# Projecting a mixer's tokens once and moving the half for the next token down a row by a transfer

## What is computed

```python
proj = u @ w_in.T                      # z, x, B, C, and the small columns dt, A, trap, angles
...
alpha = exp(A_t * dt_t)
beta  = (1 - tr_t) * dt_t * alpha      # share of the token before
gamma = tr_t * dt_t                    # share of the token itself
base  = bt * (px * beta + xt * gamma)  # px: x of the token before (0 at the first)
sr = sr * alpha + concat([base[..., :R] * cos(th), base[..., R:]])
si = si * alpha + base[..., :R] * sin(th)
y  = sum((sr[..., :R] * cos(th) + si * sin(th)) * ct[..., :R]) + sum(sr[..., R:] * ct[..., R:])
carry = (sr, si, xt)
...
out = (y + D * x) * silu(z) @ w_out.T
```

## Time and profile before

| what | value |
|---|---|
| median of 3 runs | 615.77 us (612.55 to 616.32) |
| the profiled execution | 614.08 us |
| its span in the profile | 612.4 us |
| PE busy | 557.5 us, 91% of the span |
| DVE, ACT, POOL busy | 437.5, 279.8, 229.2 us |
| mean clock of PE, of full speed | 0.974 |

### The profile page before, as it was taken

The page is one execution under the profiler, slowest core; times in us unless marked ns, Lnnn a source line. Parts: engine busy times, 40 slices in busy tenths (PEclk is TensorE's granted clock), DMA queues, the critical chain, the costliest instruction groups (busy, mean ns, idle before and its releaser), DMA issues. The chain is left out here.

```text
span 612.4 us, 17980 instructions
## 1 busy us (share of the span) xinstructions
PE 557.5 (91%) x6440; PEld 466.4 (76%) x6440; DVE 437.5 (71%) x1079; ACT 279.8 (46%) x548; POOL 229.2 (37%) x288
## 2 busy tenths in 40 slices
PE   5679999999999667999999998987999999999994
PEld 5658887888888455787788777775888888888883
DVE  2846777776787458687787787563877977977963
ACT  2357656656665324575475564453333333333220
POOL 2234246426634574325435526733031131131122
PEclk9989999999999976999999999998999999999998
DMA  7123122122211463545545638005274275265260
GB/s 227 48 85 99 42 70 69 47 63 68 61 51 35 127 188 103 151 138 149 160 131 145 162 83 231 9 7 124 52 173 113 63 172 116 61 170 113 48 155 18
DMA packets 52562, 63.21 MB, mean 103 GB/s; under 512 B 6208, under 2 KB 32480, under 8 KB 52496
## 3 DMA queue, kind: packets, MB, share of 16 engines
q1 hardware_dynamic: 50320, 59.35, 36.3%
q0 software_dynamic: 704, 1.92, 1.1%
q10 hardware_dynamic: 1472, 1.05, 0.7%
HBM read 49.26 MB, written 11.21 MB: 99 GB/s over the span
## 5 line engine op out<-in xcount | busy, mean ns | idle before, releaser
L1209 ACT ACTIVATE prob<-bank 128x512 f32<-128x512 f32 x128 | 69.4, 595 | 42.5 <-PE bank L1463 33.5
L1305 DVE TENSOR_REDUCE nmax<-bank 128x4 f32<-128x512 f32 x112 | 71.9, 684 | 22.5 <-PE bank L1463 21.1
L1998 PE MATMUL bank<-xT_hl_c,w_up 128*128 128x512 f32 x288 | 85.3, 419 | 2.9 <-ACTq L67 2.9
L1915 ACT ACTIVATE sg<-bank 128x512 f32<-128x512 f32 x72 | 43.1, 598 | 93.7 <-PE bank L1998 88.5
L2009 PEld LDWEIGHTS bank<-w_down,hid 128*128 128x128 f32 x576 | 73.9, 191 | 10.7 <-DVE hid L1955 4.4
L2009 PE MATMUL bank<-w_down,hid 128*128 128x128 f32 x576 | 76.4, 276 | 2.3 <-DVE hid L1955 1.5
L1453 PE MATMUL bank<-neg_i,mask 64*128 64x256 bf16 x512 | 51.5, 280 | 10.2 <-issue 3.4
L1998 PEld LDWEIGHTS bank<-xT_hl_c,w_up 128*128 128x128 f32 x288 | 49.5, 192 | 9.8 <-issue 3.1
L788 POOL TENSOR_TENSOR w_tok<-xg 128x256 f32<-128x256 f32 x32 | 23.8, 745 | 88.1 <-DVE xg L859 62.7
L1955 DVE TENSOR_TENSOR hid<-gu,share 128x512 f32<-128x512 f32 x64 | 47.8, 747 | 5.5 <-DMA share<-cw_scratch 3.4
L1951 DVE TENSOR_TENSOR gu<-sg,bank_pair 128x512 f32<-128x512 f32 x48 | 32.8, 683 | 22.0 <-ACT sg L1915 15.0
(11 more groups left out here) (213 smaller groups left out, 1197.2 us busy)
## 6 DMA issues: line engine op xcount, KB each, us to landing
share<-cw_scratch SPq DMA_DIRECT2D x64, 256.0 KB, 5.6
rows<-sum_rows_scratch SPq DMA_DIRECT2D x32, 256.0 KB, 3.2
k_stack<-k_scratch SPq DMA_DIRECT2D x32, 128.0 KB, 2.9
q_stack<-q_scratch SPq DMA_DIRECT2D x32, 128.0 KB, 2.8
k_scratch<-k_part SPq DMA_DIRECT2D x16, 192.0 KB, 2.4
q_scratch<-q_part SPq DMA_DIRECT2D x16, 192.0 KB, 2.4
x<-xT_in SPq DMA_DIRECT2D x8, 256.0 KB, 8.0
mask<-mask_in SPq DMA_DIRECT2D x8, 256.0 KB, 3.1
```

The costliest lines, as they stand in the source:

```text
L1209: act.activation(prob[:, b % 2, ORDER[n], :, :], (TT0, TT1)[n % 2][:, :], ACT.Exp, scale=XD ** -0.5)\
L1305: dve.tensor_reduce(nmax[:, b, 4 * u:4 * u + 4], (SS0, SS1)[n % 2][:, :].rearrange("p (i k) -> p i k", i=4), AX_X, ALU.max, negate=True).t ...
L1915: act.activation(sg[:, k, :], GG[k][:, :], ACT.Silu).then_inc(a_s.sem, 1)
L1998: mm = pe.matmul(bank[:, :], w_up[:, which, a, c, :], xT_hl[par][:, v, :], start=(n == 0), stop=(n == 2))
```

## The change

The tokens are projected once. `tokens` works on a pair q of sequences (2q, 2q + 1) with three matmuls each, and a bank holds both. DVE makes two products of 512 columns a pair: `xnext`, the tokens times the share that the next token has in them, and `w_tok`, the tokens times their own share. A DMA moves `xnext` down by one partition into `prev` (rows 0 to 126 to rows 1 to 127; row 0 of `prev` stays cleared). POOL adds `prev` to `w_tok`, 512 columns a pair. `w_tok` now holds all four sequences of a group; `prev` and `xnext` exist once.

So that DVE can multiply with the next token's share, `beta` is moved up by one row once, by a DMA of 127 rows of 512 B (`shares[:, 1]`), for which POOL makes the coefficients of the second half before the first causal selections. The cleared column of `xhl` and the wait for it go. SP issues the two moves of a group: the one of pair 1 after the first sum row of the next group, that of the next group's pair 0 after the fourth.

```diff
-        shares = sb("shares", [P, NSEQ, 2, HEADS])
-        gamma, beta = shares[:, :, 0, :], shares[:, :, 1, :]
+        shares = sb("shares", [P, 2, NSEQ, HEADS])
+        gamma, beta = shares[:, 0], sb("beta", [P, NSEQ, HEADS])
...
-        xhl = sb("xhl", [P, 2, 2, GS, P + 1], F32R)
+        xhl = sb("xhl", [P, 2, 2, GS, P], F32R)
+        prev = sb("prev", [P, 2, D_INNER])
...
-                pe.wait_ge(s_zero, 1)
...
-                dve.memset(xhl[:, :, :, :, 0:1].bitcast(F32), 0.0).then_inc(s_zero, 1)
+                dve.memset(prev[0:1, :, :], 0.0)
+                dve.memset(shares[:, 1], 0.0)
...
-        xg = sb("xg", [P, 2, 2, D_INNER])
-        w_tok = sb("w_tok", [P, 2, D_INNER])
+        w_tok = sb("w_tok", [P, GS, D_INNER])
+        xnext = sb("xnext", [P, 2, D_INNER])
...
+            sp.wait_ge(s_share, 6)
+            sp.dma_start(shares[0:P - 1, 1], beta[1:P]).then_inc(s_later, 16)
             sp.wait_ge(s_stored, 32)
+            for loaded in s_prev:
+                loaded.prime(sp)
+
+            def load_prev(g, q):
+                sp.wait_ge(s_xg.sem, s_xg.at(g, 2 * q))
+                sp.sem_inc(sp_passed, 1)
+                sp.wait_ge(s_w.sem, s_w.at(g, q - 1))
+                sp.dma_start(prev[1:P, :, :], xnext[0:P - 1, :, :]).then_inc(s_prev[q].sem, 16)
...
                 if left:
-                    for b in range(GS):
+                    load_row(sp, g + 1, 0)
+                load_prev(g, 1)
+                if left:
+                    for b in range(1, GS):
                         load_row(sp, g + 1, b)
+                    load_prev(g + 1, 0)
...
+            load_prev(0, 0)
             pairs(sp, group)
...
-            def inputs_of(g, b):
-
-                pool.wait_ge(s_xg.sem, s_xg.at(g, b))
-                pool.wait_ge(s_y.sem, s_y.at(g, b - 2))
-                pool.tensor_tensor(w_tok[:, b % 2, :], xg[:, b % 2, 0, :], xg[:, b % 2, 1, :], ALU.add).then_inc(s_w.sem, 1)
+            def inputs_of(g, q):
+
+                pool.wait_ge(s_xg.sem, s_xg.at(g, 2 * q + 1))
+                pool.wait_ge(s_prev[q].sem, s_prev[q].at(g))
+                w = w_tok[:, 2 * q:2 * q + 2, :]
+                pool.tensor_tensor(w, w, prev[:, :, :], ALU.add).then_inc(s_w.sem, 1)
...
-                inputs_of(g, 2)
-                if left:
-                    for b in range(GS - 1):
+                if left:
+                    causal(pool, g + 1, 0)
+                inputs_of(g, 1)
+                if left:
+                    for b in range(1, GS):
                         causal(pool, g + 1, b)
                 else:
                     part_third(pool, a, 0, 1)
-                inputs_of(g, 3)
-                if left:
-                    causal(pool, g + 1, GS - 1)
+                if left:
...
-                    for b in range(2):
-                        inputs_of(g + 1, b)
+                    inputs_of(g + 1, 0)
...
+            coefficients(pool, 1)
+            betas(pool, 1)
             for b in range(2):
                 causal(pool, 0, b)
-            coefficients(pool, 1)
-            betas(pool, 1)
...
-            def inputs_of(g, b):
-
-                dve.wait_ge(s_xx.sem, s_xx.at(g, b))
-                dve.wait_ge(s_w.sem, s_w.at(g, b - 2))
-                dve.tensor_tensor(xg[:, b % 2, :, :].rearrange("p s (h e) -> p (s h) e", h=HEADS),
...
+            def inputs_of(g, q):
+
+                dve.wait_ge(s_xx.sem, s_xx.at(g, q))
+                dve.wait_ge(s_prev[1 - q].sem, s_prev[1 - q].at(g - 1 + q))
+                for s, dst in ((1, xnext[:, :, :]), (0, w_tok[:, 2 * q:2 * q + 2, :])):
+                    if s == 0:
+                        dve.wait_ge(s_y.sem, s_y.at(g - 1, 2 * q + 1))
+                    dve.tensor_tensor(dst.rearrange("p b (h e) -> p (b h) e", h=HEADS),
+                                      (PX0, PX1)[q][:, :].rearrange("p (b h e) -> p (b h) e", b=2, h=HEADS),
...
-                    if b:
-                        inputs_of(g, b)
+                    if b == 1:
+                        inputs_of(g, 1)
...
-            dve.wait_ge(s_share, 6)
+            dve.wait_ge(s_later, 16)
             inputs_of(0, 0)
...
-            def tokens(g, par, b):
-
-                bank = (PX0, PX1)[b % 2]
-                pe.wait_ge(s_xg.sem, s_xg.at(g, b - 2))
-                for shift in range(2):
+            def tokens(g, par, q):
+
+                bank = (PX0, PX1)[q]
+                pe.wait_ge(s_xg.sem, s_xg.at(g - 1, 2 * q + 1))
+                for b in range(2):
                     for n, (a, v) in enumerate(((0, 0), (0, 1), (1, 0))):
-                        mm = pe.matmul(bank[:, shift * D_INNER:(shift + 1) * D_INNER], xhl[:, par, a, b, 1 - shift:P + 1 - shift],
+                        mm = pe.matmul(bank[:, b * D_INNER:(b + 1) * D_INNER], xhl[:, par, a, 2 * q + b, :],
...
             def back(g, b):
                 pe.wait_ge(s_mix.sem, s_mix.at(g, b))
-                pe.wait_ge(s_w.sem, s_w.at(g, b))
+                pe.wait_ge(s_w.sem, s_w.at(g, b // 2))
...
                 for b in range(1, GS):
-                    tokens(g, par, b)
+                    if b == 1:
+                        tokens(g, par, 1)
                     scores(g, par, b)
```

More of the change, by code:

```diff
@@ L346, in mixer @@
         rows = sb("rows", [P, GS, HEADS, P])
-        s_xx = sem("x_mm", GS)
+        s_xx = sem("x_mm", 2)
         s_g = sem("g_mm", 2 * GS)
         s_exp = sem("expo_ready", GS * HEADS)
-        s_xg, s_w = sem("xg_ready", GS), sem("w_ready", GS)
+        s_xg, s_w = sem("xg_ready", 4), sem("w_ready", 2)
+        s_prev = [sem(f"prev_loaded{q}", 1, 16) for q in range(2)]
+        sp_passed = ctx.enter_context(nc.semaphore("mixer_sp_passed"))
+        s_later = ctx.enter_context(nc.semaphore("later_shares"))
         s_mix = sem("mix_ready", GS)
@@ L354, in mixer @@
         c_rot = sb("c_rot", [P, 2, 2, GT])
-        s_zero = ctx.enter_context(nc.semaphore("x_zero_columns"))
         act_passed = ctx.enter_context(nc.semaphore("mixer_act_passed"))
@@ L377, in split_hi @@
             act.sem_inc(act_passed, 1)
-            act.activation(xhl[:, par, 0, :, 1:], xT[:, bass.ds(g * GS, GS), :], ACT.Copy).then_inc(s_hi.sem, 1)
+            act.activation(xhl[:, par, 0], xT[:, bass.ds(g * GS, GS), :], ACT.Copy).then_inc(s_hi.sem, 1)
         def steps_of(pool, g):
@@ L398, in split_lo @@
             dve.wait_ge(s_hi.sem, s_hi.at(g))
-            dve.tensor_tensor(xhl[:, par, 1, :, 1:], xT[:, bass.ds(g * GS, GS), :], xhl[:, par, 0, :, 1:].bitcast(F32),
+            dve.tensor_tensor(xhl[:, par, 1], xT[:, bass.ds(g * GS, GS), :], xhl[:, par, 0].bitcast(F32),
                               ALU.subtract)\
@@ L425, in features @@
                 for n, (i, v) in enumerate(((0, 0), (0, 1), (1, 0))):
-                    mm = pe.matmul(bank[0:m, :], w[:, i, :], xhl[:, par, v, :, 1:], start=(n == 0), stop=(n == 2))
+                    mm = pe.matmul(bank[0:m, :], w[:, i, :], xhl[:, par, v], start=(n == 0), stop=(n == 2))
                 mm.then_inc(s_feat.sem, 1)
@@ L824, in _ @@
                 causal(pool, 0, b)
-            for b in range(2):
-                inputs_of(0, b)
+            inputs_of(0, 0)
             pairs(pool, group)
@@ L853, in gates @@
                         .then_inc(s_prod.sem, 1)
-            def inputs_of(g, b):
-                dve.wait_ge(s_xx.sem, s_xx.at(g, b))
-                dve.wait_ge(s_w.sem, s_w.at(g, b - 2))
-                dve.tensor_tensor(xg[:, b % 2, :, :].rearrange("p s (h e) -> p (s h) e", h=HEADS),
-                                  (PX0, PX1)[b % 2][:, :].rearrange("p (s h e) -> p (s h) e", s=2, h=HEADS),
-                                  bc(shares[:, bass.ds(g * GS + b, 1), :, :].rearrange("p o s h -> p (o s h)")[:, :, None],
-                                     [P, 2 * HEADS, HD]), ALU.mult).then_inc(s_xg.sem, 1)
+            def inputs_of(g, q):
[6 more added lines that the diff above has]
+                                      (PX0, PX1)[q][:, :].rearrange("p (b h e) -> p (b h) e", b=2, h=HEADS),
+                                      bc(shares[:, s, bass.ds(g * GS + 2 * q, 2), :].rearrange("p b h -> p (b h)")[:, :, None],
+                                         [P, 2 * HEADS, HD]), ALU.mult).then_inc(s_xg.sem, 1)
             def group(g, par, left):
@@ L953, in skip @@
                     for n, (a, v) in enumerate(((0, 0), (0, 1), (1, 0))):
-                        pe.matmul((PY0, PY1)[k][:, :], w_dx[:, a, k * P:(k + 1) * P], xhl[:, par, v, :, 1:],
+                        pe.matmul((PY0, PY1)[k][:, :], w_dx[:, a, k * P:(k + 1) * P], xhl[:, par, v],
                                   start=(n == 0), stop=False, skip_group_check=True)
@@ L958, in back @@
                 pe.wait_ge(s_mix.sem, s_mix.at(g, b))
-                pe.wait_ge(s_w.sem, s_w.at(g, b))
+                pe.wait_ge(s_w.sem, s_w.at(g, b // 2))
                 for h in range(HEADS):
```

(2 more changed lines are left out.)

## The result

The changed kernel takes **751.17 us** (median; 746.97 to 753.69), the kernel before, run beside it, 614.82 us (612.55 to 616.32): ratio 1.2215, 95% interval 1.214 to 1.2289. The forecast was 740 us, with a range of 650 to 785. The profiled execution after has 749.59 us and a span of 747.9 us, against 614.08 and 612.4.

What follows compares the result with a forecast made beforehand. PE was taken to bound the mixer at 21.15 us a group; seven steps at 36.2 us add 105.4, the tail 18.0, the start 1.5: 124.9 on 614.08 gives 739, set to the median 740 us; range 650 to 785.

Steps and rivals of the forecast that it cites:

- One engine by equal shares: In each move, every DMA engine used takes equally many whole rows, so all 127 go to one; chance 0.82 at the rows' rate.
- fast rival: In each move, rows spread over sixteen engines, landing in 2.4 us, all covered: 606 us, faster; chance 0.11.
- twice-as-fast rival: In each move, one engine at twice the rate, landing in 7.1 us: 23.4 us a group, some 637 us; chance 0.05.
- The ring: In the mixer, two moves, two POOL sums and PE's work to the next product run serially: 2T + 9.2 = 34.2 us a group.
- the slower clock: On PE in the mixer, long waits lower the clock: 2.0 us more a group (0 to 3), making 36.2.
- T: Time of one move from issue to landing: 12.5 us, bounds 10.5 to 14.5.
- the two serial terms: In each group's loop, the second move's wait for prev to be read (1.45 us), and 6.29 us from back to product.
- Tail: After group 7's product, POOL's third part of k follows the last sum, 28.6 us after the product: +18.0 us.
- start: Before group 0's first product, beta's own move of 127 short rows queues behind two mask loads: +1.5 us (0 to 7).

Runs made afterwards that it cites:

- the half rows: The changed kernel with each move carrying only the first of the two sequences, 127 rows of 1 KB instead of 2 KB: 650.99 us in one run.
- the 124 rows: The changed kernel with 124 rows a move instead of 127, leaving out the last three rows' shares: 637.48 us, ratio 1.0343 to the kernel before.
- no move: The changed kernel without moves or waits for them, POOL adding a cleared prev: 607.21 us, ratio 0.9874 to the kernel before.
- The two moves: The changed kernel with each move made by two transfers, of 112 and 15 rows, nothing left out: 612.52 us, ratio 0.996 to the kernel before.
- the 126 rows: The changed kernel with 126 rows a move instead of 127, leaving out the last row's share: 611.66 us, ratio 0.9943 to the kernel before.

## Why the prediction was right, step by step

**One engine by equal shares** was the step on which all hung, and it held: 128 packets for 127 rows, 140 for 126, 128 for 124 and 124 for 122 are the rows and 1, 14, 4 and 2. The fast rival's condition (143 packets) isn't met. The engine's rate, doubted by the twice-as-fast rival, is 80 ns a row, against 85 worked out from the earlier trace rows.

**The ring** held with its parts: the second issue 1.29 us and `back` 1.31 us after the beginning of a sum, for twice 1.45; 8.08 us from `back` to the end of the product, for 6.29 + 2.0 with the slower clock. What the clock costs shows beside the half rows: from the second sum to the next move's issue 9.59 us go by in the kernel after (149.20 to 158.79, clock 0.73) and 7.90 in theirs (62.76 to 70.66, clock 1.00), 1.7 us for the 2.0 forecast. Their period, 25.6 us, is 2 x 8.2 + 9.2 without any, though over a whole one the clock is 0.87: it is low, 0.66, between the two sums (104.66 to 114.10), a stretch whose length the second move sets, and 1.00 behind the second (114.10 to 122.01). The sum holds for a shorter T as well. For T = 7.1 the prediction had 23.4 us a group and some 637 us (its rival of twice the rate); the 124 rows, with T about 7 for another reason, have 23.65 and 637.48.

**T was the mis-sized term**: 13.4 us in place of 12.5. The 1.7 us that aren't moving and the rate were near (1.2 us to the first row, the rest at the end; 80 ns); what was missing is that the first 19 rows of a move take 2.8 us (324.6 to 327.4), 147 ns each. xs_c, the row that was taken, couldn't show it: its eight rows an engine ran at 85 ns from the first, though nothing but one instruction load had moved in the 4 us before (416 to 420.5). So the slow start isn't a matter of the first rows alone: the transfer spread over sixteen engines hasn't got it, the one on a single engine has. In the period shown T makes 1.8 us of the 1.5 by which 37.72 is longer than the forecast 36.2; the 0.2 us from the product's end to the issue (120.87 to 121.07), which the sum left out, come on top, and the two serial terms and the 8.08 give 0.5 back. In seven steps that is the 9.9 us by which they miss the forecast (their mean is 37.62).

**Tail and start.** k's third part comes 29.7 us after the last product (337.75 less 308.03), for 28.6: T again. The start costs 0.06 us instead of 1.5: the move of `beta`, issued at 38.39 behind two mask loads, delays nothing. The tail took 0.5 us more than forecast, the start 1.4 less and the rest of the span, put at nothing, 1.7 more. That they come to under 1 us together is luck.

**The fast rival's price** was right for what it counted (606; 607.21 with no move, whose seven steps gain 6.6 us for its 7.0) and wrong for a real transfer, since it took a landing that PE doesn't wait for as covered. It looked at what waits for the sum on PE, and not at the operation of DVE that the sum would run beside. The two moves would have been 606 by it and were 612.52.

## What to carry to other kernels

Look at the slowest dimension of each transfer and not at its bytes alone: 127 rows cost 13.4 us, the same rows as 112 and 15 cost 2.9, and the whole kernel 751 or 612 us. A transfer between two steps of a pipeline moves the later step in time as well; look at what that step will then run beside, on DVE and POOL above all, before the gain is counted. A time per row read from a transfer on sixteen engines needn't hold for one on a single engine.

## What the runs showed of the hardware that wasn't expected

**A slow start.** The first 19 or 20 rows of a move on one idle engine take 147 ns each (2 KB) and 75 ns (1 KB), then 80 and 43 ns. It goes with the beginning of the movement and doesn't return for a transfer queued directly behind. Two and four engines have it too: the last move of 122 rows has 35 packets in 232.5 to 234.5 us and 50 in the next 2.0, that of 124 rows 18 in 221.2 to 222.2 and 39 in the next 1.0. Fourteen and sixteen don't show it: 54 rows of the 126 in 0.4 us (195.4 to 195.8), 104 ns each on fourteen engines, and xs_c's 85. What makes it stays open.

**An issue can be slow because of what is in front of it.** The load of xres behind a move on one engine keeps SP's queue for 3.41 us (122.46, above), and 9.62 us behind two such moves, against 0.48 us behind a move of 122 rows on two engines (221.66). One engine is not enough for it: the first load of xres in the kernel after has a move on one engine in front of it too and takes 0.41 us (46.5); what else it needs isn't shown. The loads behind it land late as well: sum rows after 9.6 us instead of 3.2, xres after 13.0 instead of 3.7 (medians). In this kernel both were hidden: of the waits in the mixer none is for xres or a sum row.

**DVE and POOL stretch each other.** 512 columns on DVE take 0.69 us alone and 1.75 beside a sum on POOL, an operation with one tensor as input 0.68 and 1.50; when DVE's begins first, the sum takes 1.82 us instead of 1.29 (the 126 rows). Not every operation of DVE is hit: `mix`, which reads a bank of PE and one tensor of SBUF, takes its 0.68 us in the middle of that sum (88.39). In the Trainium skill (SBUF — State Buffer, section "Who interferes with whom") the two engines share a pair of ports that one of them holds for a whole instruction, and the one that issues first blocks the other; the order in the timelines above agrees, the later one being the longer in each.
